# Whole first-layer steps at every second unit of a recommender tower, and the doubled sum moved to unit 10

## What is computed

```python
e = jnp.stack([tbl_f[ids[:, f]] for f in range(40)], axis=1)       # 512 x 40 x 32
z = jnp.einsum('bpd,pde,bpe->bp', e[:, i], bilinear, e[:, j])      # 780 pairs i < j
h = jnp.concatenate([z, dense_ctx], axis=1)                        # 512 x 796
h = jnp.maximum(h @ W_top1 + b_top1, 0.0)                          # 796 x 512
h = jnp.maximum(h @ W_top2 + b_top2, 0.0)                          # 512 x 256
y = h @ W_top3
```

## Time and profile before

| | us |
|---|---|
| median of 3 runs | 171.88 (171.83 to 171.97) |
| profiled execution | 172.23 |
| its span, first to last instruction | 170.4 |
| TensorE busy | 164.6 (97%) |
| VectorE busy | 144.8 (85%) |
| GpSimd busy | 112.8 (66%) |
| ScalarE busy | 42.8 (25%) |

### The profile page before, as it was taken

The page is one execution under the profiler, slowest core; times in us unless marked ns, Lnnn a source line. Parts: engine busy times, 40 slices in busy tenths (PEclk is TensorE's granted clock), DMA queues, the critical chain, the costliest instruction groups (busy, mean ns, idle before and its releaser), DMA issues.

```text
span 170.4 us, 3937 instructions
## 1 busy us (share of the span) xinstructions
PE 164.6 (97%) x1670; PEld 53.9 (32%) x1670; DVE 144.8 (85%) x144; ACT 42.8 (25%) x56; POOL 112.8 (66%) x117
## 2 busy tenths in 40 slices
PE   6799899999999999999999999999999999999993
PEld 2254344432232232332232233332232332332220
DVE  1699899998999998999999898998999999893600
ACT  3289996021000011130111210202111021111503
POOL 2777777777777777777777777777799972232000
PEclk9999999999999999999999999999999999999998
DMA  5999256987898571001016610100102550000000
GB/s 133 368 386 393 50 134 196 293 255 229 271 363 285 154 231 38 13 12 19 12 21 200 165 43 12 19 12 14 17 8 84 118 172 2 4 0 0 4 0 0
DMA packets 12890, 20.15 MB, mean 118 GB/s; under 512 B 3924, under 2 KB 6872, under 8 KB 12744
## 3 DMA queue, kind: packets, MB, share of 16 engines
q1 hardware_dynamic: 9144, 18.03, 32.0%
q0 software_dynamic: 3072, 1.58, 6.0%
q10 hardware_dynamic: 656, 0.28, 0.6%
HBM read 11.92 MB, written 0.00 MB: 70 GB/s over the span
## 4 chain that ended last, share of the span: by engine, by line
PE 87%; ACT 4%; DMA 4%; issue 2%; SPq 1%
PE y_ps L564 34%; PE z_ps L635 28%; PE t_ps L534 10%; PE y_ps L534 6%; DMA table<-hot_tables 4%; PE y_ps L578 4%; PE t_ps L578 3%; ACT plane L414 2%; PE z_ps L578 1%; ACT z_t L424 1%; PE y_ps L543 1%; SPq L356 1%; ACT xt L433 0%; ACT hot_id L475 0%; ACT xt L435 0%
## 5 line engine op out<-in xcount | busy, mean ns | idle before, releaser
L517 DVE TENSOR_TENSOR prod<-y_ps,xt 128x1024 f32<-128x1024 f32 x98 | 114.5, 1218 | 6.9 <-PE y_ps L564 4.1
L339 POOL DMA_INDIRECT x_rows<-rows,row x96 | 92.3, 961 | 29.2 <-issue 28.9
L564 PE MATMUL y_ps<-xt,m_sb 32*128 32x512 f32 x392 | 60.6, 640 | 0.0
L635 PE MATMUL z_ps<-prod,sel 128*32 128x512 f32 x392 | 51.8, 604 | 0.0
L564 PEld LDWEIGHTS y_ps<-xt,m_sb 32*128 32x128 f32 x392 | 19.1, 182 | 26.2 <-issue 17.5
L492 DVE TENSOR_SCALAR hot<-hot_id,number 128x2048 bf16<-128x2048 int16 x34 | 22.8, 744 | 4.9 <-DMA hot_id<-hot_ids 4.3
L534 PE MATMUL t_ps<-z_t,table 128*32 128x256 f32 x320 | 23.5, 379 | 0.0
L635 PEld LDWEIGHTS z_ps<-prod,sel 128*32 128x32 f32 x392 | 7.9, 108 | 36.3 <-DVE prod L517 18.9
L534 PEld LDWEIGHTS t_ps<-z_t,table 128*32 128x32 f32 x320 | 10.4, 110 | 21.4 <-issue 20.4
L578 PE MATMUL y_ps<-hot,plane 128*32 128x512 bf16 x200 | 15.2, 379 | 0.8 <-ACT plane L414 0.8
L461 ACT ACTIVATE z_t<-z_ps 128x512 f32<-128x512 f32 x6 | 3.6, 597 | 38.5 <-PE z_ps L635 36.9
(11 more groups left out here) (41 smaller groups left out, 58.6 us busy)
## 6 DMA issues: line engine op xcount, KB each, us to landing
xt<-xt SPq DMA_DIRECT2D x18, 192.0 KB, 2.5
xt<-xt SPq DMA_DIRECT2D x17, 128.0 KB, 2.4
hot_id<-hot_ids SPq DMA_DIRECT2D x4, 512.0 KB, 7.5
xt<-xt SPq DMA_DIRECT2D x32, 64.0 KB, 2.3
x_rows<-rows,row POOLq DMA_INDIRECT x96, 2.4
table<-hot_tables SPq DMA_DIRECT2D x2, 640.0 KB, 9.5
table<-w SPq DMA_DIRECT2D x1, 1280.0 KB
table<-hot_tables SPq DMA_DIRECT2D x2, 512.0 KB, 6.5
```

What stands on the lines that cost most here:

```text
L339: pool.indirect_dma_start(out=x_rows[:, g, c, :], out_offset=None, in_=rows, in_offset=bass.IndirectOffsetOnAxis(ap=row[:, n:n + 1], axis= ...
L517: nc.vector.tensor_tensor(prod[:, k % PROD_UNITS, 2 * half:2 * half + 2, :], y_ps[:, 2 * slot:2 * slot + 2, :], partners[half], ALU.mult). ...
L564: last = nc.tensor.matmul(y_ps[:, 2 * slot + place(t, u, s) % 2, :], m_sb[rows, k, :], xt[rows, moving(t, u, s), :], start=True, stop=True)
L635: last = nc.tensor.matmul(z_ps[s * DIM:(s + 1) * DIM, :], window, prod[:, k % PROD_UNITS, place(*UNIT[k], s), :], start=first, stop=(k == ...
```

## The change

Two tables of the order are rewritten. The steps of the first layer stand whole, both halves in a row, after each odd unit from 11 to 47 and after unit 48; even units from 12 to 46 have none. The sums of units 0 to 7 each stand three units behind, after units 3 to 10, and the one that makes up for it, the sum of unit 8, stands after unit 10 as well. The number of instructions and what each computes stay.

```diff
-LATE_SUMS = {2: [], 3: [0], 4: [1, 2]}
+LATE_SUMS = {2: [], **{k: [k - 3] for k in range(3, 10)}, 10: [7, 8]}
...
-TURN_STEPS = [17, 23, 31, 39]
 AFTER = {
-    "l1": sorted([*(k for k in range(11, UNITS) if k - 1 not in TURN_STEPS), *TURN_STEPS, 45, 48]),
+    "l1": sorted(2 * [*range(11, UNITS, 2), UNITS - 1]),
     "turn": [1, 10, 17, 23, 31, 39],
 }
```

## The result

The changed kernel takes 176.25 us (median of 4 runs, 176.16 to 176.5) against 171.93 before (4 runs, 171.83 to 172.23). The ratio is 1.0246, with a 95% interval of 1.0218 to 1.0273. The forecast was 176.5, in a range of 175.8 to 177.3, so the kernel is slower as forecast. Two later runs of the kernel before, 182.8 and 265.0 us, had a lower granted clock (0.90 and 0.57) and are left out of every median and ratio here.

The account below looks back on a forecast made before the run. It took TensorE as slower on average (2.50 us a unit, VectorE 2.30), the two coupled through y_ps's three slots. Terms 5.24 + 0.11 - 0.71 - 0.03 = +4.61 on 171.88 gave 176.5 us, range 175.8 to 177.3.

Parts of the forecast that it names:

- The pair: Units 12 to 47: a unit without a layer step, then one with a whole step, takes 5.37 us, against 5.00 for two with halves.
- the two diagonal surcharges: Units 16 and 30, diagonal and without a step: products start 0.20 us later, floor 2.65 instead of 2.45; net +0.11 us.
- The floor: Shortest time from a unit's start until the next unit's second half can start in a freed y_ps slot: 2.45 us.
- the rival that charged the holds to the transposes: Waits of TensorE's second halves come from VectorE's arrears after transposes, so plain units without steps cost nothing; 171.25 us, chance 0.06.
- Transposes in whole units, +0: Transposes ahead of units 17, 23, 31 and 39 cost VectorE 0.7 us each, but these units have time to spare: +0.
- The sums: Units 4 to 11: moving unit 4's second sum to unit 10 fills a wait there, a gain of 0.71 us.
- The thin cover: Sum 9 needs z's eviction, expected 0.3 us ahead of need; if it fails, up to the whole 0.71 is lost.
- The end: Unit 48: its 0.14 us loss goes, but the last sum waits for VectorE's last product, so only -0.03 us.
- The total: Whole kernel: the sum of all terms, +4.61 us, giving 176.5 us on the median of 171.88.
- The rival of cheaper whole steps: Joining two halves of a layer step saves a change of kind of matmul, 18 giving back 2.5 us; 174.0 us, chance 0.03.

Follow-up runs that it names:

- filled: The changed kernel plus 18 halves of a layer step with unused results, one in each even unit from 12 to 46; 177.41 us against 176.25.
- one_half_each: Kernel before with the changed kernel's sums and a half layer step behind every unit from 11, whole steps only at 47 and 48; 171.92 us, ratio 0.9986.
- sums_only: Kernel before with only the sums moved as in the change, layer steps left as they were; 171.56 us, ratio 0.9965.
- steps_only: Kernel before with only the layer steps moved as in the change, sums left as they were; 177.09 us, ratio 1.028.
- quarter_transposes: one_half_each with transposes cut in four: quarters spread over four units, the first two groups' ahead of one unit; 170.45 us, ratio 0.9919 to the kernel before.
- quarters_late_only: quarter_transposes with the transposes ahead of units 1 and 10 whole again, the four later ones still in quarters; 170.40 us, ratio 0.9904 to the kernel before.

## Why the prediction was right

**The pair.** Forecast 5.37, measured 5.37 at units 12 and 13. Eighteen of them and the two diagonal surcharges, 18 x 5.37 + 2 x 0.17 = 97.0, are the 97.01 of units 12 to 48. The floor that gave it, 1.17 to the product and 1.28 from there to the freed slot, was readable at four places of the old trace. All fourteen pairs without a transpose in them lasted 5.37, ten of them with none directly ahead either, so the rival that charged the holds to the transposes fell with the first profile. The old trace held a sign against it too: the holds of 0.14 behind the diagonal units stand behind no transpose. filled then showed that the hold is room and not work. No run changed the number of slots. That it is the slot for which the second half waits rests on the order in line 560 and on its start: in all 84 units from 12 on that were held by more than 0.03 us in the eight profiles, by 0.05 to 0.74, it lies 1.28 (to 0.01) behind the start of the product before it, as read from the start of the sum. one_half_each shows what was true in that rival: a whole transpose makes a hold of its own (0.45 to 0.48) behind a unit with a half step, and a whole step takes most of it in.

**Transposes in whole units, +0.** Right: units 17 to 19 split the hold, 0.08 at unit 18 and 0.30 at 19, together 0.38, that of a plain pair.

**Diagonal units.** The surcharge was put at 0.20 and measured 0.54 - 0.37 = 0.17. The forecast took it from unit 15, whose product starts 1.37 behind its matmuls. Those of units 16, 30 and 48 start 1.34 behind, in the old trace already, which gives 1.34 - 1.17 = 0.17.

**The sums.** -0.71 forecast; -0.67 by sums_only, and -0.68 by the difference of the changed kernel to steps_only. The thin cover held: sum 9 started at 55.65, directly behind unit 11's matmuls, with the copy of block 1 in time.

**The end.** -0.03 forecast, -0.04 measured. The last sum's weight loads stand 158.26 - 154.51 = 3.75 behind unit 48's start and waited for VectorE, as in the earlier trace rows, so the 0.14 at unit 48 brought nearly nothing:

```profile
158.26 0.16 PEld L634 LDWEIGHTS z_ps<-prod,sel 128*32 128x32 f32 x8 [0.80 <-DVE prod L516]
```

**The total.** +4.61 forecast, +4.58 by the distances, +4.32 by the medians. The remaining 0.26 is no step of the forecast that the traces show wrong. The sum was right for equal first phases, whose start of unit 4 varies by over 1 us between profiled executions; whether the change in medians is less for that reason alone stays open. One sign speaks for it: between the lowest times on record, 176.16 and 171.61, lie 4.55 us, though the first is the lowest of 4 runs and the second of many more. The ratio's interval, 1.0218 to 1.0273, covers 3.7 to 4.7 us.

**The rival of cheaper whole steps** has no ground: from the sum to the next unit, 61.02 to 62.88, a whole step and a sum take 1.86 = 1.00 + 2 x 0.43, as before.

## What to carry to other kernels

When two engines hand a small ring of buffers back and forth, look beside their mean loads for the shortest turn: from the start of a stage to the slot that it frees (here 1.17 + 1.28 = 2.45 us). A stage shorter than this wastes the difference each time, and a longer one does not give it back, so filler work should be spread so that each stage just clears it (2.50 here, against 2.07 and 2.93 in turn). The same holds for the other engine: its one long extra, a 0.7 us transpose, cost 0.45 in one piece and 0.05 to 0.08 in four. Here the two belonged together: spreading the steps alone gained nothing over before (one_half_each), and with the cut transposes 0.8%.

## What the runs showed of the hardware

What a transpose costs VectorE depends on what comes next. One of 128x512 is shown as 0.70 us. Where the next product reads its result, that product starts 0.74 behind it (71.87 to 72.61 before the change), and elsewhere 0.62, as ahead of unit 10 before the change:

```profile
53.92 0.70 DVE L498 STREAM_TRANSPOSE xt<-x_rows 128x512 f32<-128x512 f32 x1
54.54 1.18 DVE L517 TENSOR_TENSOR prod<-y_ps,xt 128x1024 f32<-128x1024 f32 x1
```

One of 128x128 is shown as 0.30. The next product starts 0.33 behind it where it reads the result and mostly 0.23 behind elsewhere, where it may be TensorE that it waits for. Four in a row, ahead of unit 10 in quarter_transposes, take 53.94 - 53.14 = 0.80 up to the product, against 0.62 for the whole one in the same place:

```profile
53.14 0.88 DVE L505 STREAM_TRANSPOSE xt<-x_rows 128x128 f32<-128x128 f32 x4
53.94 1.18 DVE L525 TENSOR_TENSOR prod<-y_ps,xt 128x1024 f32<-128x1024 f32 x1
```

So quarters are dearer in a row, and cheaper only where they stand in idle time.

The indirect fetches set the next bound. GpSimd issues them 1.25 us apart, 16 for a group, and the last one of the fourth group started between 83.8 and 84.0 in seven of the eight profiles. In one_half_each it is

```profile
83.96 0.95 POOL L338 DMA_INDIRECT x_rows<-rows,row  x1 [0.30 <-issue]
```

The transpose that needs it started about 2.4 us later, at 86.35 there and at 86.36 in quarters_late_only, after a wait in both. A kernel that reaches unit 23 earlier than this loses what it gained in that wait, as these two did in part.
